# Six local-attention layers on one Trainium2 core: every piece placed anew, scores in two halves, one eviction on VectorE, shifted copies of x with fewer DMAs

## What is computed

```
for i in range(DEPTH):                          # DEPTH = 6
    x = attn_layer(shift_tokens(x), Wqkv[i], q_scale[i], k_scale[i], Wo[i]) + x
    x = ffn_layer(shift_tokens(x), ln_g[i], ln_b[i], W1[i], b1[i], W2[i], b2[i]) + x

shift_tokens: the upper 64 of the 128 features are taken from the token before
attn_layer:   16 heads of 64; q and k are l2-normalised, scaled and rotated; a window of 32 tokens
              sees itself and the window before; out = softmax(8 q k^T) v, then @ Wo (1024 x 128)
ffn_layer:    layernorm, @ W1 (128 x 682), first half * gelu(second half), @ W2 (341 x 128)
```

## Time and profile before

| what | value |
|---|---|
| median of three runs | 4440.64 us (4433.11 to 4443.05) |
| the profiled execution: its own time, its span | 4443.1 us, 4441.8 us |
| PE busy | 3889.8 us, 88% of the span |
| PEld, DVE, ACT, POOL busy | 69%, 76%, 75%, 65% |
| mean granted clock of TensorE | 0.957 |
| first instruction of `phase_d` on PE | at 1400.27 us |

### The profile page before, as it was taken

One profiled execution on the slowest core, in us unless ns is written; L12 is line 12 of the kernel. 1 busy time (PEld: TensorE's weight loads), 2 busy tenths in 40 slices (PEclk: granted clock), 3 DMA queues, 4 the chain that ended last, 5 costly groups with the idle time before them and its releaser, 6 DMA issues.

```text
span 4441.8 us, 144706 instructions
## 1 busy us (share of the span) xinstructions
PE 3889.8 (88%) x60160; PEld 3060.0 (69%) x60160; DVE 3369.6 (76%) x6090; ACT 3333.1 (75%) x5144; POOL 2873.2 (65%) x2624
## 2 busy tenths in 40 slices
PE   7888466656886899999999999999999999999998
PEld 5666355545664677777787787777777777786778
DVE  4665898983555977888888788778778877887785
ACT  4665688884444887888888888778778877887786
POOL 1111788882434877777777777667667766776774
PEclk9999787888998999999999999999999999999999
DMA  2000000000000011111111111111111111111011
GB/s 63 2 2 2 1 1 1 1 1 28 2 2 20 17 24 23 31 32 29 23 32 32 23 30 25 29 31 27 24 26 27 33 27 22 34 23 25 21 24 35
DMA packets 290201, 94.92 MB, mean 21 GB/s; under 512 B 273104, under 2 KB 284560, under 8 KB 289424
## 3 DMA queue, kind: packets, MB, share of 16 engines
q1 hardware_dynamic: 289552, 85.67, 8.4%
HBM read 23.79 MB, written 2.10 MB: 6 GB/s over the span
## 4 chain that ended last, share of the span: by engine, by line
PE 74%; issue 8%; DVE 7%; POOL 5%; ACT 5%; DMA 0%; POOLq 0%; DVEq 0%; ACTq 0%; SPq 0%
PE ps L1337 15%; PE ps L1273 8%; PE ps L1325 8%; PE ps L1274 7%; PE ps L1303 6%; PE ps L1282 5%; PE ps L1379 3%; PE ps L1373 3%; PE ps L1390 3%; PE ps L1314 2%; DVE arena L617 2%; PE ps L363 2%; PE ps L1293 1%; ACT arena L512 1%; PE ps L352 1%
## 5 line engine op out<-in xcount | busy, mean ns | idle before, releaser
L1622 POOL TENSOR_TENSOR arena<-arena 128x1024 f32<-128x1024 f32 x384 | 731.5, 1905 | 576.2 <-ACT arena L1426 576.2
L1616 POOL TENSOR_TENSOR arena<-arena 128x1024 f32<-128x1024 f32 x384 | 902.6, 2372 | 12.0 <-DVE arena L1524 11.8
L1337 PEld LDWEIGHTS ps<-arena 128*128 128x128 f32 x6144 | 709.2, 192 | 13.3 <-issue 5.3
L1337 PE MATMUL ps<-arena 128*128 128x128 f32 x6144 | 717.2, 275 | 0.0
L1523 DVE TENSOR_TENSOR arena<-ps,arena 128x1024 f32<-128x1024 f32 x384 | 468.7, 1221 | 212.6 <-ACT arena L1410 206.8
L1635 POOL TENSOR_TENSOR arena<-arena 128x1024 f32<-128x1024 f32 x192 | 365.8, 1905 | 189.3 <-DVE arena L1552 189.3
L1415 ACT ACTIVATE arena<-ps 128x1024 f32<-128x1024 f32 x192 | 196.7, 1025 | 385.7 <-PE ps L1282 382.8
L227 POOL TENSOR_SCALAR arena<-arena 128x2 f32<-128x2 f32 x256 | 73.1, 286 | 613.5 <-DVE arena L221 602.2
L1524 DVE TENSOR_TENSOR arena<-ps,arena 128x1024 f32<-128x1024 f32 x384 | 465.8, 1213 | 0.0
L1410 ACT ACTIVATE arena<-ps 128x1024 f32<-128x1024 f32 x384 | 390.1, 1016 | 86.1 <-PE ps L1274 72.9
L1532 DVE TENSOR_REDUCE arena<-arena 128x32 f32<-128x2048 f32 x192 | 437.9, 2281 | 1.2 <-issue 1.2
(11 more groups left out here) (251 smaller groups left out, 8818.3 us busy)
## 6 DMA issues: line engine op xcount, KB each, us to landing
arena<-arena SPq DMA_DIRECT2D x960, 32.0 KB
arena<-in_dWqk SPq DMA_DIRECT2D x12, 512.0 KB, 4.8
arena<-arena SPq DMA_DIRECT2D x96, 64.0 KB
arena<-arena SPq DMA_DIRECT2D x96, 63.5 KB
arena<-arena SPq DMA_DIRECT2D x192, 31.5 KB
arena<-arena SPq DMA_DIRECT2D x288, 0.2 KB
arena<-in_dWvT SPq DMA_DIRECT2D x6, 512.0 KB, 4.3
arena<-in_dWo SPq DMA_DIRECT2D x6, 512.0 KB, 5.4
```

What stands on the lines that cost most here:

```text
L1337: i = pe.matmul(p[:, 0:128], o[:, u, c, :], w[:, u, c, :], start=(u == c == 0), stop=(u == 1 and c == 7))
L1616: pool.tensor_tensor(a1[:, half], a1[:, half], T2[:, half], ALU.add).then_inc(*radd[g].up())
L1622: pool.tensor_tensor(a3, a3, bc(ss[:, 16 * g:16 * g + 16], 2, 64), ALU.mult).then_inc(*nrm[g].up())
```

## The change

It does five things, all in `phase_d` and in the loads ahead of it.

1. All the numbers of `TILE`, `BATCH`, `LAYER` and `EDGE` are other ones. `s0` and `s1`, at 4686 and 4687 before, stand at 5775 and 6038, so that other pieces lie between the two halves of the scores. `wo` goes from 8266 to 10722, `fo` from 23219 to 29774.
2. `uT1`, the eviction of `u1`, goes from ACT to DVE, as a copy.
3. `xd` issues 11 DMAs, not 22; they fill partitions 0 to 63 of `XW`. A new piece, `xc`, waits for them and copies these to partitions 64 to 127 with one DMA.
4. The loads of W1 and of its biases are split into the gate's half and the other, each with a semaphore and a place of its own.
5. The load of the scales, which stood in the place of `tab` on SP, has one of its own, `lsc`.

```
-    TILE = {"radd1": 527, "radd0": 612, "q1": 781, "sq1": 1048, "q0": 1107, "ro1": 1109, "nrm0": 1119, "sq0": 1405,
...
+    TILE = {"ro1": 2176, "sq1": 2287, "sq0": 2348, "q1": 2403, "ro0": 2403, "q0": 2495, "radd1": 2557, "ssum": 2686,
+            "radd0": 2824, "rt": 3425, "nrm0": 3503, "nrm1": 3584, "halo": 4030, "kT": 4689, "t1": 4853, "qT": 4881,
+            "t0": 5027, "s0": 5775, "s1": 6038, "mx": 6110, "ex": 6599, "sum": 7085, "pn": 7368, "PT": 8777,
+            "p": 8933, "uT0": 9786, "uT1": 9825, "u0": 9980, "u1": 10021, "xxa": 10505, "wo": 10722}
+    BATCH = {"xs": 0, "sh": 190, "xd": 7112, "xc": 7632, "fd": 19214, "fst": 23153, "frs": 24297, "fn": 24855,
+             "fzT": 25361, "ft": 25539, "fge": 27008, "fg": 27177, "fgm": 28554, "fa": 28684, "xxf": 29659,
+             "fo": 29774}
...
-                pe.wait_ge(*xw[m % 2].at(352 * (m // 2 + 1)))
+                pe.wait_ge(*xw[m % 2].at(192 * (m // 2 + 1)))
...
-            if piece in ("uT0", "uT1"):
+            if piece == "uT0":
...
+            if piece == "uT1":
+                if n >= 2:
+                    dve.wait_ge(*S.wo_ps.at(n - 1))
+                dve.wait_ge(*S.u1_ps.at(n + 1))
+                dve.tensor_copy(UT[n % 2][:, :, :, 64:128],
+                                ps("u1", n).rearrange("p (u c q) -> p u c q", u=2, c=8)).then_inc(*S.uT1.up())
...
-            if piece == "lw1":
+            if piece == "lwg":
+                sp.wait_ge(*S.fg_ps.at(NB * l))
+                sp.dma_start(w1[:, DI:2 * DI], d["dW1"][l][:, DI:2 * DI]).then_inc(*L.ld_wg.dma())
+            if piece == "lwa":
                 sp.wait_ge(*S.fa_ps.at(NB * l))
-                sp.dma_start(w1, d["dW1"][l]).then_inc(*L.ld_w1.dma())
+                sp.dma_start(w1[:, 0:DI], d["dW1"][l][:, 0:DI]).then_inc(*L.ld_wa.dma())
...
-                for u in range(2):
-                    w = XW[m % 2][64 * u:64 * u + 64]
-                    sp.dma_start(w[0:32, 1, 0, 0:64], x[96:128, 0, 0:64]).then_inc(*got.dma())
...
+                w = XW[m % 2]
+                sp.dma_start(w[0:32, 1, 0, 0:64], x[96:128, 0, 0:64]).then_inc(*got.dma())
...
+            if piece == "xc":
+                m = l * NB + k
+                got, w = xw[m % 2], XW[m % 2].rearrange("p t k f -> p (t k f)")
+                sp.wait_ge(*got.at(192 * (m // 2) + 176))
+                sp.dma_start(w[64:128, :], w[0:64, :]).then_inc(*got.dma())
```

More of the change, by code:

```diff
@@ L1221, in phase_d @@
     FB = [(stats(C), sb([128, 2]), sb([128, 2, 128]), sb([128, 2, 128]), sb([128, 3, 256])) for _ in range(NF)]
-    TILE = {"radd1": 527, "radd0": 612, "q1": 781, "sq1": 1048, "q0": 1107, "ro1": 1109, "nrm0": 1119, "sq0": 1405,
[3 rows of a table removed]
[L1227 to L1231, removed]
+    TILE = {"ro1": 2176, "sq1": 2287, "sq0": 2348, "q1": 2403, "ro0": 2403, "q0": 2495, "radd1": 2557, "ssum": 2686,
[3 rows of a table added]
+    BATCH = {"xs": 0, "sh": 190, "xd": 7112, "xc": 7632, "fd": 19214, "fst": 23153, "frs": 24297, "fn": 24855,
+             "fzT": 25361, "ft": 25539, "fge": 27008, "fg": 27177, "fgm": 28554, "fa": 28684, "xxf": 29659,
+             "fo": 29774}
+    LAYER = {"lsc": 5000, "tab": 16000, "lvo": 8000, "wv0": 15930, "wv1": 15931, "we0": 16774, "we1": 16775,
+             "lqk": 33442, "lln": 55694, "lwg": 57319, "lwa": 58623, "lbg": 57421, "lba": 58971, "lw2": 59920}
+    EDGE = {"e0": 31545, "e1": 32702, "e2": 34584, "e3": 34595, "out": 37210}
     order = [(1000 * (NT * l + k) + t, piece, l, k) for piece, t in TILE.items() for l in range(depth) for k in range(NT)]
@@ L1376, in batch @@
             if piece == "fa":
+                if b == 0:
+                    pe.wait_ge(*L.ld_wa.at(16 * l + 16))
                 p = claim("fa", m)
@@ L1480, in batch @@
                 if b == 0:
-                    act.wait_ge(*L.ld_b1.at(16 * l + 16))
+                    act.wait_ge(*L.ld_bg.at(16 * l + 16))
                 if m < NF:
@@ L1563, in batch @@
             if piece == "fgm":
+                if b == 0:
+                    dve.wait_ge(*L.ld_ba.at(16 * l + 16))
                 dve.wait_ge(*S.fge.at(m + 1))
@@ L1684, in load @@
                 sp.dma_start(wo, d["dWo"][l]).then_inc(*L.ld_vo.dma())
-            if piece == "lw1":
+            if piece == "lwg":
+                sp.wait_ge(*S.fg_ps.at(NB * l))
+                sp.dma_start(w1[:, DI:2 * DI], d["dW1"][l][:, DI:2 * DI]).then_inc(*L.ld_wg.dma())
+            if piece == "lwa":
                 sp.wait_ge(*S.fa_ps.at(NB * l))
-                sp.dma_start(w1, d["dW1"][l]).then_inc(*L.ld_w1.dma())
+                sp.dma_start(w1[:, 0:DI], d["dW1"][l][:, 0:DI]).then_inc(*L.ld_wa.dma())
+            if piece == "lbg":
+                sp.wait_ge(*S.fge.at(NB * l))
+                sp.dma_start(b1[:, 3:6], d["db1"][l][:, 3:6]).then_inc(*L.ld_bg.dma())
+            if piece == "lba":
+                sp.wait_ge(*S.fgm.at(NB * l))
+                sp.dma_start(b1[:, 0:3], d["db1"][l][:, 0:3]).then_inc(*L.ld_ba.dma())
             if piece == "lln":
@@ L1693, in load @@
                 sp.dma_start(w2, d["dW2"][l]).then_inc(*L.ld_w2.dma())
-            if piece == "lb1":
-                sp.wait_ge(*S.fgm.at(NB * l))
-                sp.dma_start(b1, d["db1"][l]).then_inc(*L.ld_b1.dma())
-            if piece == "tab":
+            if piece == "lsc":
                 sp.wait_ge(*S.tab.at(l))
@@ new lines, in sp_program @@
+                sp.dma_start(w[0:64, :, 1, 0:64], x[0:64, :, 0:64]).then_inc(*got.dma())
+                sp.dma_start(w[1:64, :, 1, 64:128], x[0:63, :, 64:128]).then_inc(*got.dma())
+                sp.dma_start(w[0:64, :, 2, 0:64], x[32:96, :, 0:64]).then_inc(*got.dma())
+                sp.dma_start(w[0:64, :, 2, 64:128], x[31:95, :, 64:128]).then_inc(*got.dma())
+                sp.dma_start(w[0:64, :, 3, 0:64], x[64:128, :, 0:64]).then_inc(*got.dma())
+                sp.dma_start(w[0:64, :, 3, 64:128], x[63:127, :, 64:128]).then_inc(*got.dma())
@@ L1829, in load_d @@
     C.top = C.TOTAL - LAST
-    L = C.loads("ld_rope ld_sc ldd_q ldd_k ldd_vo ldd_w1 ldd_w2 ldd_b1 ldd_ln")
+    L = C.loads("ld_rope ld_sc ldd_q ldd_k ldd_vo ldd_wg ldd_wa ldd_w2 ldd_bg ldd_ba ldd_ln")
     wqk, wvT, wo, w1, w2 = sb([128, 2048]), sb([128, 8, 128]), sb([128, 8, 128]), sb([128, 682]), sb([128, 3, 128])
```

27 lines of the change are left out of this document (12 added, 15 removed), and 3 rows, old and new, of the table TILE.

## The result

The changed kernel takes 4394.05 us (median of 4 runs, 4388.09 to 4400.39), the kernel before beside it on the same chip 4436.88 us. The ratio is 0.9906, with an interval of 0.9881 to 0.9930: faster by 0.9%, 43 us. The forecast was 4350, a gain of 91 us; the result lies inside the range (4280 to 4455), but more than half of the gain is missing. The profiled execution has a span of 4391.6 us, 50.2 less than before (4441.8), at a mean granted clock of 0.954 (before 0.957).

What follows compares the result with a forecast made beforehand. The prediction took PE to bound the kernel. Its terms summed to -91 us, from the profiled 4443.1 us to 4352, less 2.5 for the median of the runs 4349.5, given as 4350, with a range of 4280 to 4455.

Steps and rivals of the forecast that it cites:

- Halts: PE's standstills before the scores, 126.1 us over the run: scores in halves would remove three quarters, -95 us.
- Rival B: At the scores, halts not tied to run length only move: 4459 us; chance 0.10 with the half-stay case (4400).
- Clock: PE's clock dips after standstills, some 19 us; with three quarters of the halts gone -14, between -19 and 0.
- The change part by part: The prediction's section that prices each part of the change in turn, its terms summing to -91 us.
- Load of the next q and k: On SP behind `xd` and `fd`, lands late for next layer's `q1`: up to 2 us, five times, +5 us.
- Fill: Deeper pipeline before the first `wo`: one more tile of `q` costs at most 11.3 us; taken as +5.
- Switches: On PE, two more switches between kinds of matmul a tile, +38 us, against faster scores, -29; taken as +5.
- `uT1` on DVE: DVE's added copy, 1.2 us, brings it to 93% without making PE wait; +3 us before the FFN's first batch.
- rival A: DVE hands over late to PE: 1.2 us a tile, 4578 us, half of it 4464; chance 0.15, at about 4480.
- DMAs and W1: Loads of x with fewer `xd` issues and split loads of W1: both covered, nothing gained or lost.
- rival C: Before the scores all halts go, and the scores run faster: -161 us, so 4280; chance 0.12.

Runs made afterwards that it cites:

- e1_fold: Changed kernel with the evictions of the folded weights, `we0` and `we1`, at 15750 and 15751 in place of 16774 and 16775: 4320.63 us, ratio 0.9717.
- e2_lqk: Changed kernel with the load of the next q and k weights at 33100, ahead of `xd`, in place of 33442: 4376.45 us, ratio 0.9847.
- e3_both: Changed kernel with both edits, those of e1_fold and e2_lqk, together: 4298.22 us, ratio 0.9666.
- b1_split: Kernel before with `s1` at 4790 in place of 4687, so that only `q1` lies between the halves of the scores: 4413.92 us, ratio 0.9950.
- e4_unsplit: Changed kernel with the scores in one piece again, `s1` at 5776 in place of 6038: 4525.15 us, ratio 1.0185.
- e7_best_dma22: e3_both with the 22 DMAs per tile of before and no `xc`: 4300.78 us, ratio 0.9684.
- b2_dma: Kernel before with the fewer DMAs alone, `xd` with 11 issues and `xc` at 5200: 4420.74 us, ratio 0.9974.

## Why the prediction promised twice the gain

From 1400 us to the end, worked out from the windows' span and PE busy time:

| kernel | span | PE busy | PE idle |
|---|---|---|---|
| before | 3041.8 | 2875.9 | 165.9 |
| changed | 2991.6 | 2899.3 | 92.3 |
| e1_fold | 2922.1 | 2875.4 | 46.7 |
| e2_lqk | 2973.1 | 2896.6 | 76.5 |
| e3_both | 2899.0 | 2866.1 | 32.9 |

**Halts, -95 of 126.** Under-sized: all 126 went, in the changed kernel, e1_fold, e3_both and b1_split. What the mechanism (a store that a run of short records empties) says comes out: the halts end with the halves while the DMA packets stay (b1_split), they keep the period of two packets in every trace that has them, and they move when the neighbours move (e4_unsplit). The store itself no run shows. Rival B, with the rule of the page "Runtime: NRT & Kernel Launch" of the Trainium skill (section on instruction fetch mechanics) that fetching is hidden, falls: the same 481 packets cost 126.1 us in one order and 0.2 in another. That the packets in question are PE's is still an inference, from their count and the period.

**Clock, -14.** Wrong sign. The step looked only at dips that end with the halts. Dips summed as (1 - granted clock) x 50 us over the windows from 1550 to 4250 are 18.5 us before, 30.5 after, 10.0 in e1_fold and 0 in e3_both, so all that the term could bring was there, and the clusters and the late load took it.

**The step that failed: the fold had no term.** "The change part by part" prices what is named in the diff's five points and treats the new numbers as an order of pieces on engines. They also hand out PSUM. That `we0` moved from 0.09 to 0.84 of a turn behind `wv0` was in the diff's numbers, and no line of the sum asks who holds a buffer for long. What the runs showed in its place: five clusters of waits, one behind each fold, in which nine pieces of PE in a row use one buffer. Their price is the step from the changed kernel to e1_fold: 45.6 us of idle time, five times 9.1, and 23.9 us of busy time at the lower clock, 69.5 in the spans.

**Load of the next q and k, +5.** The place was right ("up to 2 us, five times"), the size 18 in place of 5. The wait is 14.5 us in five pieces of 2.4 to 3.8. The 14 issues ahead of the load took 12.6 to 13.0 us, within the 13.4 allowed, and PE went on 19.5 to 20.8 us after the end of the `u1` that released `xd`, near the 18 to 20 allowed; but `q1` was due after 17.1 to 17.3 us and not 18, and the term took 1 us of the gap a time where 3 came. The lower clock behind it comes on top.

**Fill, +5, bounds 0 and +8.** The first weight load of `wo` starts at 1492.3, before at 1481.0, so 11 us later (1495.1 in e3_both), and from the last one to the end are 47.6 us in place of 36.8. This moves work as the prediction says, and its net cost wasn't measured by itself. The filling takes one turn of DVE after the other; its `ssum` starts in e3_both:

```profile
1453.51 2.27 DVE L1535 TENSOR_REDUCE arena<-arena 128x32 f32<-128x2048 f32 x1
...
1486.72 2.28 DVE L1535 TENSOR_REDUCE arena<-arena 128x32 f32<-128x2048 f32 x1
```

Three turns lie between them, 11.1 us each, in which DVE doesn't wait, and the term had looked to POOL's 11.3.

**Switches, +5 of -29 to +38.** Two tiles take 0.18 us more than the earlier trace rows, 0.09 a tile, +17 us if all do: inside the bounds, on the dear side. The two groups of scores, 329.5 us against 319.1, don't run faster.

**`uT1` on DVE, +3.** Right that PE doesn't wait for a DVE at 92%, and rival A falls. What the move brings is 8 us here, not clear of noise, and 16 once nothing else stands in the way (13.7 in the spans), where the prediction had a cost of 3.

**DMAs and W1, 0.** Right for the fewer packets where there are no halts (e7_best_dma22). The split of W1's load and the place of `lsc` weren't tried by themselves.

**In sum**: rival C (4280, all halts gone) was the nearest picture of what the change has to give: mended, it takes 4298, though the scores don't run faster. As it was, the five places of the fold took 73 us and the load 18. In the spans e3_both is 142.8 us below the kernel before. The prediction's terms without the load give 96; the halts bring 31 more, the clock 4.5, `uT1` 17, the switches 12 less, which makes 136. That the result still lies inside the range is partly luck: what the halts, the clock and `uT1` brought above their price covers half of the 92.6 us that the two places took.

## What to carry to other kernels

When a table of numbers sets the order, list for each shared buffer who holds it from when to when, in the kernel before and after, once for the steady turn and once for each place that comes seldom (a layer's first tile, a load): 126 us gained all along the block stood against some 91 lost at two places that come once a layer. Groups of waits with the same small count point to such a place, and the timeline there, read beside the list of who holds which buffer, shows that it is one buffer. A run of very short instructions is worth breaking with longer work, if the pieces put between find their buffers free.

## What the chip showed beyond this

- Waits of 1.0 to 1.5 us in a row, some one to two us of work apart, bring PE down from 2.4 to 1.2 GHz in the cluster above: the window from 2000 us has a granted clock of 0.90, and a pair of `q` takes 2.04 us there and 1.02 at 2098 us. The single halts of up to 2.4 us before the change, 82 in all, left a lower clock in 11 of 54 windows only.
- The halts inside runs of short matmuls keep a distance of 249 to 251 matmuls, or a multiple of 125, whatever piece they fall into (the kernel before and e4_unsplit; the longest miss of a multiple is 11, at 3386).
- The halts may get shorter with fewer small DMA packets beside them: 1.54 to 1.44 us each with about a third less of them (b2_dma, one trace each). What links the two wasn't tried.
- DVE at 46 to 47 of 50 us in e3_both makes PE wait for it 1.9 us in all from 1550 us on.
